# A graph network's edge batches: node numbers shared by groups of four, and gathers that wait for a free buffer alone

## The reference

```python
edge_index = jnp.stack([src, dst])
h = jnp.maximum(_layernorm(x), 0.0)
# L0: attention with 8 heads of 32, row = src, col = dst
q, k, v = h @ Wq + bq, h @ Wk + bk, h @ Wv + bv      # q also times 32 ** -0.5
s = jnp.einsum('ehd,ehd->eh', q[row], k[col])
p = jnp.exp(s - segment_max(s, row)[row])
attn = p / segment_sum(p, row)[row]
x = x + segment_sum(attn[:, :, None] * v[col], row).reshape(n, 256) @ Wo + bo
# L1: sum of the edge features of each dst, and a three-layer perceptron
h = jnp.maximum(_layernorm(x), 0.0)
aggr = segment_sum(edge_attr_256, edge_index[1])
h = relu(relu(concatenate([h, aggr]) @ W1 + b1) @ W2 + b2) @ W3 + b3
return x + h
```

## Time and profile before

| | |
|---|---|
| median of three runs | 1962.83 us (1957.73, 1962.83, 1965.74) |
| profiled execution, its span | 1958.7 us; no time of its own beside the span is recorded |
| instructions in the profile | 25681 |
| mean granted clock of PE | 0.886 of full speed |
| moved by DMA | 459.28 MB, 234 GB/s over the span |

### The profile page before, as it was taken

One profiled execution on the slowest core, in us unless ns is written; L12 is line 12 of the kernel. 1 busy time (PEld: TensorE's weight loads), 2 busy tenths in 40 slices (PEclk: granted clock), 3 DMA queues, 4 the chain that ended last, 5 costly groups with the idle time before them and its releaser, 6 DMA issues.

```text
span 1958.7 us, 25681 instructions
## 1 busy us (share of the span) xinstructions
PE 1489.4 (76%) x6687; PEld 1107.9 (57%) x6687; DVE 1514.7 (77%) x2769; ACT 928.9 (47%) x2828; POOL 957.8 (49%) x1006
## 2 busy tenths in 40 slices
PE   4799988477767777767777777777777565699998
PEld 4545556355556555656556656565555443476664
DVE  9997978687787778787878787878787897676663
ACT  5644457355555555545455555455545111254442
POOL 6001018465666666666666666566656666322210
PEclk7799999798898988888889888888898887899999
DMA  8023447698888888888889888888898777343321
GB/s 208 26 105 128 160 152 261 215 311 286 297 299 299 295 303 299 296 304 298 303 296 307 294 303 298 304 296 302 298 295 296 235 229 211 109 121 106 105 90 37
DMA packets 237272, 459.28 MB, mean 234 GB/s; under 512 B 46857, under 2 KB 147878, under 8 KB 237120
## 3 DMA queue, kind: packets, MB, share of 16 engines
q0 software_dynamic: 72288, 236.33, 35.4%
q1 hardware_dynamic: 138376, 132.97, 21.0%
q10 hardware_dynamic: 26456, 88.28, 14.1%
HBM read 385.03 MB, written 72.44 MB: 234 GB/s over the span
## 4 chain that ended last, share of the span: by engine, by line
PE 33%; another core or an unknown queue 23%; ACT 21%; DVE 10%; issue 9%; DMA 2%; POOL 0%; SPq 0%; ACTq 0%; DVEq 0%; POOLq 0%
ACT EBO L855 8%; ACT EBO L857 7%; PE bank L1120 5%; PE bank L1215 5%; PE bank L1393 4%; PE bank L1092 3%; PE bank L1414 2%; PE bank L1093 2%; PE bank L1402 2%; PE bank L1376 2%; DVE V L1461 2%; DVE EBO L1461 2%; PE bank L1095 2%; ACT R L865 1%
## 5 line engine op out<-in xcount | busy, mean ns | idle before, releaser
L722 POOL DMA_INDIRECT U<-kv_rows,dstb x856 | 814.8, 952 | 506.8 <-issue 241.5
L1120 PE MATMUL bank<-EBO 128*128 128x256 f32 x1568 | 442.9, 430 | 296.6 <-ACT R L865 260.8
L1120 PEld LDWEIGHTS bank<-EBO 128*128 128x128 f32 x1568 | 322.7, 213 | 376.0 <-issue 317.8
L1760 DVE TENSOR_TENSOR V<-U,bank_pair 128x1024 f32<-128x1024 f32 x214 | 260.3, 1216 | 97.5 <-issue 52.6
L857 ACT ACTIVATE EBO<-EBO,ones 128x128 f32<-128x128 f32 x728 | 292.4, 402 | 29.1 <-issue 3.2
L1215 PE MATMUL bank<-V 128*128 128x264 f32 x1136 | 291.3, 401 | 11.7 <-DVE V L1801 7.3
L855 ACT ACTIVATE EBO<-iota,dA 128x128 f32<-128x128 f32 x728 | 286.7, 394 | 0.5 <-issue 0.3
L1215 PEld LDWEIGHTS bank<-V 128*128 128x128 f32 x1136 | 228.4, 201 | 56.1 <-DVE V L1801 8.2
L1801 DVE TENSOR_TENSOR V<-U,bank 128x1024 f32<-128x1024 f32 x142 | 172.5, 1215 | 79.6 <-ACT bank L919 54.1
L1764 DVE TENSOR_REDUCE V<-V 128x32 f32<-128x1024 f32 x142 | 173.3, 1220 | 4.9
L1215 PE MATMUL bank<-U 128*128 128x264 f32 x576 | 157.7, 422 | 8.2 <-ACT V L933 8.1
(11 more groups left out here) (310 smaller groups left out, 2214.8 us busy)
## 6 DMA issues: line engine op xcount, KB each, us to landing
EBO<-in_edge_attr_dram ACTq DMA_DIRECT2D x163, 512.0 KB
V<-q_rows SPq DMA_DIRECT2D x128, 128.0 KB
EBO<-in_edge_attr_dram SPq DMA_DIRECT2D x31, 512.0 KB
o_log<-R SPq DMA_DIRECT2D x108, 132.0 KB
o_log<-V SPq DMA_DIRECT2D x106, 132.0 KB
U<-kv_rows,dstb POOLq DMA_INDIRECT x856
kv_rows<-U SPq DMA_DIRECT2D x49, 256.0 KB, 2.0
ag_rows<-R SPq DMA_DIRECT2D x98, 128.0 KB
```

The costliest lines, as they stand in the source:

```text
L722: e.indirect_dma_start(out=kvb[:, b % NKV, j, :], out_offset=None, in_=kv_dram[:, :], in_offset=bass.IndirectOffsetOnAxis(ap=dstb[:, k:k + ...
L1120: m = e.matmul(agg_bank(c)[:, 0:D], oh2[i][0:n, j, :], eb[h % NEB][0:n, j % 4, :], start=j == 0, stop=j == 7)
L1760: e.tensor_tensor(T1, kvb[:, b % NKV, :, 0:D], qv, ALU.mult).then_inc(b_mult, 1)
```

## The change

Four batches of a group now share one base, the first node of the group. For that the group must span at most 128 nodes and no node may have more than 128 edges; the flag `more` now tells of this as well, is known before the first batch, and every engine branches on it there. With the flag set the old code runs, otherwise `grouped_rounds`:
- One query load a group (`group_q`, 54 instead of 214), with three buffers; the expansions stay one a batch.
- PE sums all 16 products of a group in one bank (3 + g % 2); ACT copies it once and SP writes it once, to `g_log` (132 KB each, 54 instead of 214). The last row of the group before, if its node goes on, is added by one more product with a column of `sel`; that product waits for ACT's copy of the group before.
- The maxima take in 32 positions (HALO) of the neighbouring batches' rows on each side, so all parts of a node in a group and its neighbours have the same maximum. The chain for group g runs after the scores of batch 4g + 4, with six first transposes instead of four, scans over 160 columns and a copy of two columns of maxima carried on. Weighting lags LG = 5 batches instead of 4. The scores stand in a ring of 12 batches, so that the steps of one chain in three are split in two parts. Borders are made for two groups at once by three products each.
- Gathers wait for their buffer alone; there are NKG = 10 of them. The four batches whose gathers stand ahead of the branch keep the old buffers' numbers.
- The repair at the end and its transfers run in the old branch only. SP signals after the last log write and then loads `pa`; POOL starts on the tiles at that signal. The zero fill of the unused end of `o_log` (4092 KB, early in the kernel) is gone. Row masks are three instead of six.

```diff
+        NGR = NBT // SG
+        NKG = 10
+        NQG = 3
+        HALO = 32
+        WS = P + 2 * HALO
+        DEG = 4 * HALO
...
+        LG = LAG + 1
...
-            def gather(b):
+            def gather(b, n):
...
-                if b >= NKV + VB:
-                    e.wait_ge(b_pv, b - NKV + 1)
-                if b >= VB + 6:
-                    e.wait_ge(b_qe, b - 1)
+                if b >= n + VB:
+                    e.wait_ge(b_pv, b - n + 1)
...
+            def group_q(g):
+                if g >= NQG:
+                    e.wait_ge(b_qe, SG * (g - NQG + 1))
+                r = e.value_load(nqi[0:1, SG * g:SG * g + 1], min_val=0, max_val=NP) if g else 0
+                e.dma_start(qg[g % NQG], q_dram[bass.ds(r, P), :] if g else q_dram[0:P, :]).then_inc(s_q[g % NQG], 16)
+
+            def group_rows(g):
+                e.wait_ge(b_ev, g + 1)
+                e.dma_start(g_log[g * P:(g + 1) * P, :], Rg[g % NR]).then_inc(s_o[g % NR], 16)
...
+                grouped_rounds()
+                e.sem_inc(sp_over, 1)
                 load_sums()
...
+                for b in range(VB + len(early), NBT):
+                    gather(b, NKG)
+                border_sums()
+                border_sums_back()
+                e.wait_ge(sp_over, 1)
+                e.wait_ge(tv.s, T_ZC)
+                tiles_in(g_log, NGR * P)
...
+            def group_rows(g):
+                e.wait_ge(b_o, SG * (g + 1))
+                if g >= NR:
+                    e.wait_ge(s_o[g % NR], 16 * (g // NR))
+                e.copy(Rg[g % NR], bank[3 + g % 2][:, 0:RW]).then_inc(b_ev, 1)
...
+            def group_borders(z):
...
+                for i in range(NZ2):
+                    o = bank[2][0:SG * NH, P + i * WS:P + (i + 1) * WS]
+                    before, own_, behind = (nrepG[:, SG * i + k:SG * i + k + SG].rearrange("p b h -> p (b h)") for k in range(3))
+                    e.matmul(o, own_, diffG[:, :], start=True, stop=False)
+                    e.matmul(o[:, 0:HALO + 1], before, diffG[:, P:P + HALO + 1], start=False, stop=False)
+                    t = e.matmul(o[:, HALO + P:WS], behind, diffG[:, HALO:2 * HALO], start=False, stop=True)
...
+            def group_expand(b):
+                g = b // SG
+                e.wait_ge(g_oh, g + 1)
+                e.wait_ge(s_q[g % NQG], 16 * (g // NQG + 1))
+                if b >= 2:
+                    e.wait_ge(b_mult, b - 1)
+                e.matmul(bank[b % 2][:, 0:D], ohTg[g % 2][:, b % SG, :], qg[g % NQG], start=True, stop=True).then_inc(b_qe, 1)
+
+            def group_weighted(b):
+                g, y = divmod(b, SG)
+                o = bank[3 + g % 2]
+                first = b == max(g * SG, VB)
+                e.wait_ge(b_pv, b + 1)
+                e.wait_ge(b_pl, b + 1)
+                if first and g >= 2:
+                    e.wait_ge(b_ev, g - 1)
+                for j in range(4):
+                    if y == SG - 1 and j == 3 and g:
+                        e.wait_ge(b_ev, g)
+                        e.matmul(o[0:1, 0:RW], sel[:, g:g + 1], Rg[(g - 1) % NR], start=False, stop=False)
+                    t = e.matmul(o[:, 0:RW], ohog[b % NPV], PVg[b % NPV][:, j, :, :].rearrange("p h d -> p (h d)"),
+                                 start=first and j == 0, stop=y == SG - 1 and j == 3)
+                t.then_inc(b_o, 1)
...
+            def group_chain(g):
+                lo, hi = SG * g + 1 if g else 0, min(SG * g + SG + 1, NBT)
+                i = g % 2
+                e.wait_ge(b_red, hi)
+                if g:
+                    step(e.tensor_copy(M6[:, 0:2, :], M6[:, SG:SG + 2, :]))
...
+                cut = min(hi, (lo // RING + 1) * RING)
+                parts = [(a, b) for a, b in ((lo, cut), (cut, hi)) if a < b]
...
+                for q in range(0, P, 32):
+                    dv.on(e.transpose(MTg[0:32, HALO + q:HALO + q + 32], M6[q:q + 32, 1:SG + 1, :].rearrange("p b h -> p (b h)")))
+                dv.on(e.transpose(MTg[0:32, 0:HALO], M6[P - 32:P, 0:SG, :].rearrange("p b h -> p (b h)")))
+                dv.on(e.transpose(MTg[0:32, HALO + P:WS], M6[0:32, 2:SG + 2, :].rearrange("p b h -> p (b h)")))
...
+                dv.on(e.tensor_tensor_scan(MFg[0:32, :], ngz[:, 0:HALO + P], MTg[0:32, 0:HALO + P], -BIG, ALU.add, ALU.max))
```

More of the change, by code:

```diff
@@ L557, in first_loads, with sums_out @@
                     load_q(b)
+            def sums_out(b):
+                for k in range(agg_by_batch(b - 1) if b > VB else AGG0, agg_by_batch(b)):
+                    if k % 8 == 6 and k > 8:
+                        agg_out(e, k // 8 - 1)
+                    if k == AGG_STEPS - 1:
+                        agg_out(e, k // 8)
             def rounds(lo, hi, first, last):
@@ L730, in pool_program @@
                 e.wait_ge(s_kvo[i], 16 * ((NT + 1 - i) // 2))
-            for b in (VB, VB + 2, VB + 1, *range(VB + 3, NBT)):
-                gather(b)
+            early = (VB, VB + 2, VB + 1, VB + 3)
+            for b in early:
+                gather(b, NKV)
+            e.wait_ge(flags_ready, 1)
+            more_ = e.value_load(more[0:1, 0:1], min_val=0, max_val=1)
             def rows_in(tile, dram, n, at):
@@ L773, in pool_program @@
+            pl.n = n0
+            with e.Else():
+                for b in range(VB + len(early), NBT):
+                    gather(b, NKG)
+                border_sums()
+                border_sums_back()
+                e.wait_ge(sp_over, 1)
+                e.wait_ge(tv.s, T_ZC)
+                tiles_in(g_log, NGR * P)
             if NT > NF:
@@ L1172, in tensor_program @@
             e.wait_ge(row_in, 2)
-            e.matmul(bank[3][0:1, 0:1], bad[:, 5:6], ones[:, 0:1], start=True, stop=True).then_inc(row_out, 1)
+            for i, k in enumerate((5, 4)):
+                t = e.matmul(bank[3][0:1, i:i + 1], bad[:, k:k + 1], ones[:, 0:1], start=True, stop=True)
+            t.then_inc(row_out, 1)
             e.wait_ge(row_in, 3)
@@ new lines, in group_places, with grouped_rounds @@
+            def group_places(p):
+                e.wait_ge(row_in, 4 + p)
+                e.wait_ge(a_ev, NCH)
+                for t in range(p * MT3, min(NT, p * MT3 + MT3)):
+                    m = e.matmul(bank[6][:, t:t + 1], msk[p % 2][:, 0, t - p * MT3, :], dDb[:, 0:1], start=True, stop=True)
+                m.then_inc(row_mm, 1)
+            def grouped_rounds():
+                for g in range(3):
+                    q_side(g)
+                group_expand(VB)
+                group_expand(VB + 1)
+                for b in range(VB, NBT + LG + 2):
+                    if b == FARB:
+                        far_rows()
+                    if b in places_at:
+                        group_places(places_at[b])
+                    if b == SPAN + 1:
+                        group_turns()
+                    if b + 2 < NBT:
+                        group_expand(b + 2)
+                    if b == VB + LG + 1:
+                        e.wait_ge(span_out, 2)
+                    if VB <= b - LG - 1 < NBT:
+                        group_weighted(b - LG - 1)
+                    if b in ng_at:
+                        group_borders(ng_at[b])
+                    g, y = divmod(b + 1, SG)
+                    if y == 2 and 0 < g < NGR - 2:
+                        q_side(g + 2)
+                    sums(b)
```

568 lines of the change are left out of this document (403 added, 165 removed).

## The result

The changed kernel takes 2120.05 us (median of four runs, 2103.57 to 2130.52) beside 1964.22 us of the kernel before: 1.0788 times as long, 95% interval 1.0754 to 1.0822 (the 1962.83 us ahead of the prediction are the median of three of the four runs of the kernel before). I had forecast 1893 us; the time is outside my range of 1790 to 2060. It is rival (c), at the price named there.

The account below looks back on a forecast made before the run. No engine alone bounds the batch stage; POOL's gather runs and pauses set its pace, PE bounds the output stage. 1958.7 - 66 (batches) - 1 (end) = 1892, 1896 as median, 1893 with fewer small DVE waits; range 1790 to 2060 us.

Parts of the forecast that it names:

- rival (c): Batch stage: the removed gather wait was useful, DVE stalls longer in each chunk; 2050 to 2190 us, mild form from 1985; 29%.
- Sum: Batch stage: pace 4.94 + pause/run gives 5.77 us a batch instead of 6.08, saving 66 us over 214 batches.
- the late stretch: Last batches, without edge sums: POOL runs four batches long, pauses of 3.85 us, 5.90 us a batch; used against rival (c).
- What is late next is PE's bank of edge sums: Gathers: once the wait on expansions falls, the next late thing is PE's edge-sum bank; direct price 40.4 us and part of 171.7.
- DVE +0.2 us a batch: Batch stage: the new chain adds about 0.8 us a group on DVE, 0.2 a batch.
- start 0: Before the first batch: flag, branch and small DVE steps cost nothing, bounds -5 and +8 us.
- end -1: After the batches: 12 us of repair go, the edge-sum load comes later; -4 to +3 us, taken as -1.
- DMA bytes worth nothing: Batch stage: 41.6 MB fewer in query loads and log writes save nothing by themselves, DMA being under the other floors.
- the grouped branch taken: Branch before the first batch: a group spans some 117 nodes against 128 allowed, so the grouped code runs.
- DVE's floor 5.1 us: Batch stage: DVE's least time a batch, 4.9 us before the change, 5.1 after it.
- For PE I said +0.2 us a batch: Batch stage: carry row and wider borders raise PE's busy time from 4.5 to 4.7 us a batch.
- Rival (a): Batch stage: POOL never needs to pause, DVE bounds at 5.1 to 5.3 us a batch; 1755 to 1795 us; 15%.

Follow-up runs that it names:

- session 3: Runs on one chip with PE results seen late: kernel before 1946.54 us; changed kernel with gathers' wait on expansions restored and two edge-sum banks 1926.99 us, 0.9903.
- two banks: Changed kernel with gathers' wait on expansions restored and two PSUM banks for edge sums during the batches: 0.9903 with PE results late, 1.0119 without.
- the brake: Gathers' wait until PE has expanded the batch two before; put back alone in the changed kernel: 1953.27 us, 0.9985 times the kernel before.
- session 1: Runs on one chip with PE results seen late: kernel before 1956.52 us; changed kernel with only the gathers' wait on expansions restored 1953.27 us, 0.9985.
- session 2: Runs without late PE results: kernel before 1727.63 us; changed kernel with gathers' wait on expansions restored and two edge-sum banks 1749.19 us, 1.0119.
- half rows: Changed kernel with gathers of 1 KB rows instead of 2 KB, values left out: 1730.42 us (1.0010) without late PE results, 2080.55 us (1.0699) with them.

## Why the prediction was wrong

**The step that failed** is in "Sum": "a batch costs 4.94 + 3.3/4 = 5.77 us". The form held (4.94 + pause/run), and so did the run: 66 waits in 214 batches are 3.2 batches a run, within my three to five. What failed is the pause. I took its 3.3 us from pauses that a release of PE's results ends, though the edit takes just that wait away. After it POOL is started by DVE's weighting, which stands behind a release, the scores and at times a chain: 419.1/66 = 6.35 us on average, 11.65 in the cycle shown. 3.3/4 = 0.8 us a batch became 419.1/214 = 2.0.

**Rival (c)** had the mechanism with its steps: POOL goes on by a further batch, then the pause, then everyone resumes. I gave 6.75 us for DVE's stall (6.3 on average, 7.32 shown) and 2050 to 2190 us (2120.05); how the stall's growth was shared out over the chunks, which gave that range, no run tested. I gave it 29%, since the late stretch, four batches a run at 5.90 us, seemed to clear long runs of blame. But there the wait on expansions still started POOL again. A run of three or four batches is harmless where a release ends the pause after it, as in session 3 with two banks; what costs is a pause that DVE must end.

**"What is late next is PE's bank of edge sums"**: half right. With the brake two banks are worth about 0.8% (0.9903 in session 3 beside 0.9985 in session 1).

**Right were the small terms:** DVE +0.2 us a batch (4.76 to 4.95); start 0 (+0.8 between the first scores); end -1 (-1.6), with the tile gathers early and the edge sums late; DMA bytes worth nothing in a stage that they don't bind (459.28 to 411.75 MB, 47.5 less; the logs and queries are 42.6 of them, as 160 x 260 KB of 1024 bytes, where I wrote 41.6); the grouped branch taken; DVE's floor 5.1 us, which the kernels of session 2 reach (5.12 and, with half rows, 5.03). For PE I said +0.2 us a batch; it is 220.53/300 x 6.86 - 4.47 = 0.57, with its clock at 0.83 instead of 0.87 and products drawn out while results are held; what part each has wasn't separated.

**Rival (a)**, DVE-bound at 5.1 to 5.3 us, is nearly what session 2, not held, shows for the unbraked kernel of half rows (5.03 us). There also the kernel before is fast, so the edit could gain little. The Trainium skill's "Trainium Architecture — The Big Picture", section "What this means for kernel authors", says that a matmul on TensorE doesn't block a copy on VectorE unless a semaphore stands between the two; the one contention between engines that it names is a pair of ports that VectorE and GpSimd share. In the sessions that weren't held the traces agree: no wait ends with "remote". In the held ones an expansion that by the profile had ended at 898.45 us reached DVE only at 912.47, 2.4 us after a gather's end, and a rest of 2 us on POOL alone gave back most of the loss; so there the measurement goes against that rule. The shared ports can't be all of it, since ACT waits for PE's results as well (337.5 us at L1058).

**Open:** what in the chip carries the hold, and why a session has it or not. The profile models the ends of PE's products, so it can't tell a late signal from a product that really ended late; that PE's own entries come slowly in these stretches fits either. Also how the changed kernel itself does where nothing is held: it never ran there. A rest of 2 us with two banks was not tried where results are held.

**The best version** where results are held is the grouped kernel with the brake and two banks for the edge sums, 0.9903 times the kernel before. Where they aren't, no kernel that ran was faster than the kernel before.

## What to carry to other kernels

A wait can be a brake: before removing one, ask not only what it costs but what will start the engine again in its place, and how long that chain is. Take the price of a pause from a pause that ends in the way that the changed kernel's will. When a profile shows "remote" waits that end together just after another engine's run of gathers, compare both kernels on the same chip at the same time, since the same kernel can take 12% less at another (1728 us beside 1957).

## What the runs showed of the hardware

- The kernel before took 1946 to 1957 us in three sessions and 1728 us in two, once on the same chip. In the slower kind PE's results reach ACT, DVE and POOL late while POOL issues gathers. Most come through some 2 to 3 us after the last gather (912.5 after 910.1), a part of them inside a run. 2.0 us between gathers after every 8 gave most of the loss back (1.0130), 0.6 us more than usual gave nothing that shows. Halving the gathers' bytes left the loss (1.0699).
- While results are held PE also issues slowly: at 902 to 912 us of the changed kernel entries of 0.6 us start 1.4 us apart, and SP's write of a chunk's sums at 907.27 takes 0.72 us to issue, where 0.36 is the median of these writes in the same kernel and 0.37 the longest in session 2 with half rows.
- With nothing held the grouped kernel with brake and two banks runs at 5.12 us a batch with DVE busy 97% of the time; the same kernel with held results runs at 5.92, with DVE busy 82%.
